# Second layer of a four-layer attention kernel: turns of one pair of heads of both batches, turned probabilities in the scores' banks

## The chip, the cores and the metric

The kernel runs on one core of a Trainium2 chip. The metric is the device time of one execution in microseconds (us); several runs are made, and their median is given.

## The reference

Four cross-attention layers run one after another over `x` of shape (16, 128, 256), each with the same context `ctx_2048` of that shape. The change touches the second layer alone. It handles 16 batches with 16 heads of 64 rows each; its weights differ for the first and the second half of the 256 columns:

```python
for i in range(len(IDX_LIST)):                      # columns 0:128 and 128:256
    s, e = (bounds[i], bounds[i + 1])
    h = jnp.einsum('od,bdl->bol', Wq_list[i], z1ss[:, :, s:e])
    h = h + jnp.einsum('od,bdl->bol', Wi_list[i], u1ss[:, :, s:e])
    chunks.append(h)
w_heads = jnp.concatenate(chunks, axis=2)
q, k, v = jnp.split(w_heads, 3, axis=1)             # 16 heads of 64 rows each
rq = q + r_w_bias[None, :, :, None]
score = jnp.einsum('bndi,bndj->bnij', rq, k) * SCALE
prob = jax.nn.softmax(score, axis=-1)
attn_vec = jnp.einsum('bnij,bndj->bndi', prob, v)
attn_vec = attn_vec.reshape(bsz, N_HEAD * D_HEAD, qlen)
attn_out = jnp.einsum('od,bdl->bol', Wo, attn_vec) + bo[None, :, None]
x = attn_out + z1ss
m = jnp.mean(x, axis=1, keepdims=True)
var = jnp.var(x, axis=1, keepdims=True)
return (x - m) * jax.lax.rsqrt(var + LN_EPS)
```

The first layer (self attention, cross attention and an MLP) runs before it; the third and fourth layers run after it and overlap its end.

## The kernel before, in words

The second layer is `layers123`, and every engine has a program of its own in it that waits on counted semaphores. The 16 batches go in 8 **rounds** of NB = 2 batches. A round has PAIRS = 8 pairs of heads, and STEPS = 16 **steps**: step t handles pair t // 2 of batch t % 2, so each step is two heads of one batch.

What happens to one step, with the function that does it and its line:

- `project` (L1797 for v, L1799 for q and k, on TensorE, PE in the profile) makes q and k of a pair for both batches, or v of four heads for one batch. Each call is 12 matmuls over the full 128 x 128 array, of 256 columns each. The values that are multiplied are split into a rounded part and a rest ("h" and "l" in the tiles' names), hence three products for each one. ScalarE (ACT) rounds q and k out of PSUM into `qh`, `kh` (`round_work`, L1954, L1957), VectorE (DVE) makes the rests (`rest_work`, L2045, L2049) and copies v (L2040). Two PSUM banks, 6 and 7, take these projections and the small matmuls of the layer norm in turn (`work`).
- `scores` (L1813): 12 matmuls per step, each with 64 rows of the array, those of the two heads at the same time in the two halves. They go to `score_bank`, PSUM banks 0 and 1, one for each head.
- `maxima` (L2018, DVE), `exponentials` (L1934, ACT, with the sums), `inverse_sums` (L2024, DVE), `norm` (L1739, GpSimd, POOL).
- `turn` (L1825): 8 transposes of 128 x 128 blocks of the probabilities, over the full array, into `turn_bank`, banks 2 and 3. `copy_turned` brings them to `pT`: head 0 on ACT (L1943), head 1 on DVE (L2029).
- `times_v` (L1841): the probabilities times v, each matmul with 64 columns of the array, the two heads at the same time, into `pv_bank`, half of bank 4. ACT rounds the result (`round_heads`, L1949), DVE makes its rest (`rest_heads`, L2034).
- `times_wo` (L1850): once a pair, three matmuls of 512 columns into bank 5, which adds up over the whole round.

TensorE's order is written by hand in `body`: in step t, `scores(t)`, `times_v(t - 2)`, `turn(t - 1)`, in even steps `times_wo` of the pair two behind, and then the calls that the table `FILLS` names for the step, one to three of them. These fills are the projections of the next pair and the layer norm of the round before: "mean" (L1859), "var" (L1866) and "inv0", "inv1" (`spread`, L1874). `T_Y`, `T_READ`, `T_DIAG` and `T_ZU` are the steps in which the other engines do the round's extra work: adding the residual, the inverse root, the diagonal, and splitting the next round's inputs into `zu` (L1963 and L1968 on ACT, L2055 and L2060 on DVE). In the first round ACT, DVE and POOL also split the weights in parts (`round_part`, `rest_part`).

Since the scores of every step use the same two banks, `scores(t)` waits until the exponentials of step t - 1 have been read:

```python
pe.wait_ge(*exp_done.at(i, 2 * t - 1))
```

`turn(t)` waits for `norm` of its step and for `copy_turned` of step t - 1, `times_v(t)` for both `copy_turned` of its step and for `rest_heads` of step t - 1.

Of the kernel before, what the change touches and what calls it, by code (L numbers as in the profile page):

```python
# [9 lines left out]
F32 = mybir.dt.float32  # L10
# [5 lines left out]
P = 128  # L16
B = 16
D = 256
# [1537 lines left out]
def layers123(nc, v):  # L1556
# [8 lines left out]
    RE = 2  # L1565

    L_T, L_V, L_W = 1, 2, 4
    SCALE = HD1 ** -0.5
    with ExitStack() as ctx:
# [33 lines left out]
        q = [sb(f"q{p}", [P, 2, 2, NB, P], F32R) for p in ("h", "l")]  # L1603
        k = [sb(f"k{p}", [P, 2, 2, NB, P], F32R) for p in ("h", "l")]
        vs = sb("vs", [P, 2, NB, 2, 4 * HD1])
        prob = sb("prob", [P, RE, 2, BANK])
        pT = sb("pT", [P, 2, BANK])
# [51 lines left out]
        FILLS = [("q1", "k1"), ("v0b1", "q2"), ("k2",), ("v1b0", "q3"), ("k3", "v1b1"), ("q4", "mean"), ("k4",),  # L1659
                 ("v2b0", "q5", "var"), ("k5",), ("v2b1", "q6"), ("k6", "v3b0"), ("q7", "k7"), ("v3b1", "inv0"),  # L1660
                 ("inv1",), ("q0+", "k0+"), ("v0b0+",)]
        T_Y, T_CENTRE, T_READ, T_DIAG, T_ZU = 2, 6, 8, 9, 13
# [14 lines left out]
        pv_done = event("pv_done", STEPS)  # L1677
        aT_hi = event("aT_hi", STEPS)
        aT_lo = event("aT_lo", STEPS)
# [7 lines left out]
        joins = {"work_free": [work.out(n, R1 - 1) for n in ("inv0", "inv1")], "product_free": y_done.at(R1),  # L1687
                 "scores_free": ((exp_done.at(R1 - 1, 2 * STEPS - 1),),
                                 tuple(copied[h].at(R1 - 1, STEPS - 1) for h in range(2)))}
# [15 lines left out]
        def tile_of(name):  # L1705
            slot = int(name[1]) % 2
            if name[0] == "v":
                return vs[:, slot, int(name[3]), :, :].rearrange("p c f -> p (c f)")
            return [w[:, slot, :, :, :].rearrange("p c b l -> p (c b l)") for w in (q if name[0] == "q" else k)]
# [25 lines left out]
        def _(pool):  # L1735
# [18 lines left out]
            def body(i, first, last):  # L1754
                for t in range(STEPS):
                    for h in range(2):
                        norm(i, t, h)
                    if first and t < len(PARTS) - AT_ONCE:
                        rest_part(t + AT_ONCE)
                    if t == T_READ:  # L1760
                        inverse_std(i, "var")
# [18 lines left out]
        def _(pe):  # L1780
# [21 lines left out]
            def scores(i, t):  # L1802
# [422 lines left out]
```

## Time and profile before

| What | Value |
|---|---|
| median of 3 runs | 1278.05 us (1273.24 to 1278.2) |
| the profiled execution's own time | 1274.89 us |
| its span | 1273.2 us |
| busy in the span: PE, DVE, ACT, POOL | 95%, 73%, 65%, 43% |
| first and last matmul of `scores` start at | 466.5 and 1188.7 us |

The span is what the hardware profiler recorded of the core, and 1.7 us lie around it. A PE row gives the time at which a matmul starts and a modelled length that overlaps the next one: matmuls of a steady stream start 0.11 to 0.12 us apart while each is listed with 0.28 us. Whether TensorE lost time is therefore read from the starts. "x8" in a row of the timeline means that eight like instructions are merged, and the time is that of all of them.

### The profile page before, as it was taken

What the parts mean: (1) busy time and instruction counts of PE and PEld (TensorE: products, weight loads), DVE (VectorE), ACT (ScalarE), POOL (GpSimd) and SP (SyncE); (2) the same over time, 40 slices, a digit from 0 to 9 for tenths busy, and PEclk for the clock granted to TensorE, in tenths of its full rate; (3) what the DMA queues carried; (4) which work ended last, traced back from release to release, by engine and by line L of the source; (5) the groups of instructions that cost most, each with busy time, mean ns of one, the idle gap of its engine ahead of it and who ended that gap; (6) DMA issues with size and microseconds to landing.
All of it is one profiled execution on the core that took longest, in us unless ns stands there. A gap on an engine that the chain in (4) does not pass through costs nothing.

```text
span 1273.2 us, 29851 instructions
## 1 busy us (share of the span) xinstructions
PE 1204.5 (95%) x10914; PEld 989.7 (78%) x10914; DVE 927.0 (73%) x1835; ACT 825.9 (65%) x2523; POOL 547.2 (43%) x535
## 2 busy tenths in 40 slices
PE   4789999999999889999999999999999999999997
PEld 3667787788887678888888888888888888888675
DVE  4778989889898658767676766767667676766564
ACT  4688978978986658565655565565565656655542
POOL 4455655556643236433333334333334334333443
PEclk8999999999999999999999999999999999999999
DMA  3350000000000000000000000000000100000011
GB/s 108 101 211 16 10 22 9 12 12 17 6 14 1 1 25 2 1 10 2 1 10 2 9 2 1 10 1 2 9 2 2 55 1 2 1 2 1 18 42 42
DMA packets 18575, 25.39 MB, mean 20 GB/s; under 512 B 1424, under 2 KB 17040, under 8 KB 17936
## 3 DMA queue, kind: packets, MB, share of 16 engines
q1 hardware_dynamic: 18448, 23.69, 5.6%
q8 instruction: 81, 1.33, 0.4%
q14 instruction: 46, 0.38, 0.1%
HBM read 21.58 MB, written 2.10 MB: 19 GB/s over the span
## 4 chain that ended last, share of the span: by engine, by line
PE 51%; ACT 6%; DVE 3%; issue 2%; DMA 0%; POOL 0%; ACTq 0%; SPq 0%
PE psum L1797 12%; PE psum L1841 9%; PE psum L1825 9%; PE psum L1813 7%; PE psum L1799 5%; ACT prob L1934 3%; PE psum L1850 3%; ACT pT L1943 1%; PE psum L1322 1%; PE psum L1386 1%; DVE l_neg_max L2018 1%; DVE aTl L2034 1%; PE psum L1866 1%; PE psum L1336 1%; ACT aTh L1949 1%
## 5 line engine op out<-in xcount | busy, mean ns | idle before, releaser
L1739 POOL TENSOR_TENSOR prob<-prob,l_z_inv 128x512 f32<-128x512 f32 x256 | 261.0, 1040 | 439.1 <-DVE l_z_inv L2024 439.1
L1934 ACT ACTIVATE prob<-psum,l_neg_max 128x256 f32<-128x256 f32 x512 | 235.5, 472 | 225.7 <-DVE l_neg_max L2018 225.7
L794 ACT ACTIVATE ring_e<-ring_e,neg_max 128x128 f32<-128x128 f32 x512 | 164.2, 406 | 15.0 <-DVE neg_max L973 14.9
L2018 DVE TENSOR_REDUCE l_neg_max<-psum 128x2 f32<-128x512 f32 x256 | 163.8, 681 | 10.7 <-PE psum L1813 10.6
L1825 PEld LDWEIGHTS psum<-ident,prob 128*128 128x128 f32 x1024 | 109.8, 141 | 50.3 <-issue 45.4
L1841 PE MATMUL psum<-pT,vs 128*64 128x256 f32 x1024 | 138.8, 391 | 3.7 <-DVE aTl L2034 3.5
L1825 PE MATMUL psum<-ident,prob 128*128 128x128 f32 x1024 | 140.2, 280 | 1.0 <-POOL prob L1739 1.0
L478 POOL TENSOR_TENSOR ring_e<-ring_e,cross_add 128x512 f32<-128x512 f32 x64 | 85.2, 1348 | 90.4 <-DVE ring_e L968 90.4
L2029 DVE COPY pT<-psum 128x512 f32<-128x512 f32 x128 | 88.0, 687 | 45.6 <-PE psum L1825 45.4
L478 POOL TENSOR_TENSOR ring_e<-ring_e,self_add 128x512 f32<-128x512 f32 x64 | 85.9, 1356 | 62.6 <-DVE ring_e L968 61.9
L2034 DVE TENSOR_TENSOR aTl<-psum,aTh 128x256 fp32r<-128x256 f32 x128 | 54.3, 424 | 74.6 <-ACT aTh L1949 74.6
L802 ACT COPY ring_t<-psum 128x512 f32<-128x512 f32 x128 | 75.2, 588 | 45.7 <-PE psum L645 44.9
L1934 ACT ACTIVATION_READ_ACCUMULATOR prob<-psum,l_neg_max 128x1 f32 x512 | 103.9, 203 | 0.0
L1841 PEld LDWEIGHTS psum<-pT,vs 128*64 128x64 f32 x1024 | 63.6, 136 | 39.6 <-issue 7.3
L645 PE MATMUL psum<-ident,ring_e 128*128 128x128 f32 x512 | 81.6, 283 | 10.3 <-ACT ring_t L802 9.3
L1813 PE MATMUL psum<-kh,qh 64*128 64x256 f32 x512 | 85.8, 329 | 5.4 <-ACT prob L1934 5.4
L645 PEld LDWEIGHTS psum<-ident,ring_e 128*128 128x128 f32 x512 | 61.5, 144 | 34.4 <-issue 13.3
L973 DVE TENSOR_REDUCE neg_max<-ring_e 128x4 f32<-128x512 f32 x128 | 84.7, 673 | 2.3 <-POOL ring_e L478 2.3
L1943 ACT COPY pT<-psum 128x512 f32<-128x512 f32 x128 | 76.3, 596 | 0.2 <-PE psum L1825 0.2
L1813 PE MATMUL psum<-kl,qh 64*128 64x256 f32 x512 | 72.8, 278 | 0.0
L1813 PE MATMUL psum<-kh,ql 64*128 64x256 f32 x512 | 72.5, 276 | 0.0
L1797 PE MATMUL psum<-zuh,wzl 128*128 128x256 f32 x256 | 72.2, 282 | 0.0
(208 smaller groups left out, 3169.9 us busy)
## 6 DMA issues: line engine op xcount, KB each, us to landing
wz_raw<-wz_in SPq DMA_DIRECT2D x2, 1536.0 KB, 14.6
wi_raw<-wi_in SPq DMA_DIRECT2D x2, 1536.0 KB, 19.2
x_in<-x SPq DMA_DIRECT2D x8, 256.0 KB, 2.7
cT<-ctxT SPq DMA_DIRECT2D x8, 256.0 KB, 2.8
w<-w_in SPq DMA_DIRECT2D x2, 1024.0 KB, 8.9
l_ub<-ctx_in SPq DMA_DIRECT2D x8, 256.0 KB, 3.2
cg<-ctx_in SPq DMA_DIRECT2D x4, 512.0 KB, 4.1
out<-fin SPq DMA_DIRECT2D x8, 256.0 KB, 2.2
```

The costliest lines, as they stand in the source:

```text
L478: pool.tensor_tensor(e, e, add, ALU.add).then_inc(scores_add.sem, 1)
L645: last = nc.tensor.transpose(turn_bank[:, h * P:(h + 1) * P], ring_e[:, n % RE, h * P:(h + 1) * P], ident[:, :])
L794: last = nc.scalar.activation(e, e, ACT.Exp, bias=neg_max[:, n % RE, h:h + 1])
L1739: pool.tensor_tensor(e, e, z_inv[:, t % RE, h, :].unsqueeze(2).broadcast_to([P, 2, D]), ALU.mult)\
L1797: last = mm(o, w, zu[xp][:, s, c, :, :].rearrange("p b l -> p (b l)"), **flags)
L1813: last = mm(score_bank[h][:, qt * D:(qt + 1) * D], q[qp][rows, pair % 2, qt, b, :], k[kp][rows, pair % 2, :, b, :], start=(qp, kp) == (0, ...
L1825: last = nc.tensor.transpose(turn_bank[h][:, kt * D + qt * P:kt * D + (qt + 1) * P], prob[:, t % RE, h, qt * D + kt * P:qt * D + (kt + 1) ...
L1841: last = mm(pv_bank[h * HD1:(h + 1) * HD1, :], vs[:, pair // 2 % 2, b, kt, at:at + HD1], pT[:, h, kt * D:(kt + 1) * D], start=kt == 0, sto ...
L1934: last = nc.scalar.activation(prob[:, t % RE, h, qt * D:(qt + 1) * D], score_bank[h][:, qt * D:(qt + 1) * D], ACT.Exp, bias=neg_max[:, t % ...
L1943: nc.scalar.copy(pT[:, 0, :], turn_bank[0]).then_inc(copied[0].sem, 1)
L2018: nc.vector.tensor_reduce(neg_max[:, t % RE, h, :], score_bank[h].rearrange("p (t c) -> p t c", t=2), AX.X, ALU.max, negate=True).then_inc ...
L2029: nc.vector.tensor_copy(pT[:, 1, :], turn_bank[1]).then_inc(copied[1].sem, 1)
```

## The change

A round now has 8 **turns** n, one for each pair of heads, each with both batches. The scores of batch 0 go to banks 0 and 1 and those of batch 1 to banks 2 and 3. There are no banks of their own for the turned probabilities: `turn` of pair n - 1 and batch b writes into the banks in which the scores of pair n and batch b stood, once the exponentials have read them. The order on TensorE in turn n is: `scores(n, 0)`, `scores(n, 1)`, `times_v(n - 2)` for both batches, the first fill, `turn(n - 1, 0)`, the second fill, `times_wo(n - 2)`, `turn(n - 1, 1)`, the other fills. `pv_bank` is the whole of bank 4, so `round_heads` and `rest_heads` run once a pair over 512 columns. `prob` has four slots (RE = 4) and `pT` one for each batch; `q` and `k` have one slot in place of two. The other engines' orders follow. Where the last round meets the third layer, the waits name the new events, and `queries_keys3` and `values3` come after the last turn.

```diff
-    RE = 2
+    RE = 4
...
-        score_bank = [psum[:, j, :] for j in range(2)]
-        turn_bank = [psum[:, 2 + j, :] for j in range(2)]
-        pv_bank = psum[:, 4, 0:D]
+        score_bank = [[psum[:, 2 * b + h, :] for h in range(2)] for b in range(NB)]
+        pv_bank = psum[:, 4, :]
...
-        T_Y, T_CENTRE, T_READ, T_DIAG, T_ZU = 2, 6, 8, 9, 13
+        FILLS = [("q1", "k1", "v0b1"), ("q2", "k2", "v1b0"), ("q3", "k3", "v1b1", "mean"),
+                 ("q4", "k4", "v2b0", "var"), ("q5", "k5", "v2b1"), ("q6", "k6", "v3b0", "inv0"),
+                 ("q7", "k7", "inv1", "v3b1"), ("q0+", "k0+", "v0b0+")]
+        T_Y, T_READ, T_DIAG, T_ZU = 1, 3, 4, 6
...
+            def scores(i, n, b):
...
-                pe.wait_ge(*exp_done.at(i, 2 * t - 1))
+                for h in range(2):
+                    pe.wait_ge(*copied[h].at(i, NB * (n - 2) + b))
...
+            def turn(i, n, b):
+                t = NB * n + b
                 for h in range(2):
                     pe.wait_ge(*probs_done.at(i, 2 * t + h))
-                    pe.wait_ge(*copied[h].at(i, t - 1))
...
+                        pe.wait_ge(*exp_done.at(i, 2 * (t + NB) + h))
...
+            def body(i, first, last):
+                for n in range(PAIRS):
+                    f = fills(i, n, last)
+                    scores(i, n, 0)
+                    scores(i, n, 1)
+                    if n >= 2 or not first:
+                        times_v(*behind(i, n, 2))
+                    fill(f[0:1])
+                    if n >= 1 or not first:
+                        turn(*behind(i, n, 1), 0)
+                    fill(f[1:2])
...
+                        times_wo(*behind(i, n, 2))
+                    if n >= 1 or not first:
+                        turn(*behind(i, n, 1), 1)
+                    fill(f[2:])
...
+                    exponentials(i, n, 0, 0)
+                    exponentials(i, n, 0, 1)
+                    if n >= 2 or not first:
+                        round_heads(*behind(i, n, 2))
+                    if f:
+                        round_work(f[0][1], f[0][0])
+                    exponentials(i, n, 1, 0)
+                    if n >= 1 or not first:
+                        copy_turned(*behind(i, n, 1), 0)
+                    exponentials(i, n, 1, 1)
+                    if f:
+                        round_work(f[1][1], f[1][0])
+                    if n >= 1 or not first:
+                        copy_turned(*behind(i, n, 1), 1)
```

How the instructions stand on TensorE in a middle round (`kh,qh` and the like are `scores`, `pT,vs` is `times_v`, `ident,prob` is `turn`, `wzh` and `zuh` are projections, `woh` is `times_wo`). A step before:

```order
L1813 MATMUL psum<-kh,qh 128x256 [waits l1_exp_done]
...
L1813 MATMUL psum<-kh,ql 128x256 x2
L1841 MATMUL psum<-pT,vs 64x256 [waits l1_pT1_copied,l1_aT_lo,l1_pT0_copied,l1_work_bank1_read_out]
L1841 MATMUL psum<-pT,vs 64x256 x3
L1825 MATMUL psum<-ident,prob 128x128 [waits l1_pT0_copied,l1_probs_done]
```

A turn after the change, up to the first transposes:

```order
L1820 MATMUL psum<-kh,qh 128x256 [waits l1_pT0_copied,l1_pT1_copied,l1_work_bank0_read_out,l1_work_bank1_read_out]
...
L1820 MATMUL psum<-kh,qh 128x256 [waits l1_pT1_copied,l1_pT0_copied]
...
L1820 MATMUL psum<-kh,ql 128x256 x2
L1853 MATMUL psum<-pT,vs 64x256 [waits l1_pT1_copied,l1_pT0_copied,l1_aT_lo]
...
L1801 MATMUL psum<-zuh,wzh 128x256 [waits l1_work_bank0_read_out,l1_zu_lo,i_weights_lo_made,z_weights_lo_made]
...
L1836 MATMUL psum<-ident,prob 128x128 [waits l1_exp_done,l1_probs_done]
```

The sequence scores, times v, full array came twice a pair and comes once; the scores no longer wait for exponentials, and the transposes now do.

ScalarE (ACT) in a middle turn after the change, from `round_heads` to the second `copy_turned`:

```order
L1971 CAST aTh<-psum 128x512 [waits l1_wo_done,l1_pv_done]
L1976 ACTIVATE qh<-psum,cols 128x512 [waits l1_work_bank1_full]
L1957 ACTIVATE prob,l_z_sum<-psum,l_neg_max 128x256 [waits l1_turned,l1_max_done]
...
L1966 COPY pT<-psum 128x512 [waits l1_pv_done,l1_turned]
L1957 ACTIVATE prob,l_z_sum<-psum,l_neg_max 128x256 [waits l1_turned,l1_max_done]
...
L1979 ACTIVATE kh<-psum 128x512 [waits l1_work_bank0_full]
L1966 COPY pT<-psum 128x512 [waits l1_pv_done,l1_turned]
```

The rounding of q, which waits for its projection, now stands in front of the two exponentials of batch 1; before, the rounding of q or k closed a step.

## Rows read from the trace of the kernel before

**Rows 1.** Windows: stretch and length, busy PE, PEld, DVE, ACT, POOL, PEclk, DMA, GB/s
```profile
863.00:954.00 91.00, 89.79 (x777) 75.24 (x777) 62.63 (x133) 53.46 (x177) 33.59 (x33) 1.00 0.02 5
```

**Rows 2.** Timeline of PE (start, us, line): the "mean" of two rounds
```profile
863.53 1.02 PE L1859 MATMUL psum<-l_y,mean_w 128*128 128x512 f32 x2
...
954.87 1.02 PE L1859 MATMUL psum<-l_y,mean_w 128*128 128x512 f32 x2
```

**Rows 3.** Timeline of PE, one step without a stall
```profile
852.41 0.28 PE L1797 MATMUL psum<-zul,wih 128*128 128x256 f32 x1
852.53 0.28 PE L1797 MATMUL psum<-zuh,wil 128*128 128x256 f32 x1
852.74 0.39 PE L1813 MATMUL psum<-kh,qh 64*128 64x256 f32 x2
852.96 0.28 PE L1813 MATMUL psum<-kl,qh 64*128 64x256 f32 x2
...
853.43 0.28 PE L1813 MATMUL psum<-kh,ql 64*128 64x256 f32 x2
853.64 1.08 PE L1841 MATMUL psum<-pT,vs 128*64 128x256 f32 x8
854.66 1.09 PE L1825 MATMUL psum<-ident,prob 128*128 128x128 f32 x8
855.51 0.47 PE L1850 MATMUL psum<-aTh,woh 128*128 128x512 f32 x1
...
856.28 0.28 PE L1797 MATMUL psum<-zuh,wzh 128*128 128x256 f32 x1
```

**Rows 4.** The same step, asked for in shorter windows: later starts in `times_v`
```profile
853.91 0.60 PE L1841 MATMUL psum<-pT,vs 128*64 128x256 f32 x4
...
854.12 0.60 PE L1841 MATMUL psum<-pT,vs 128*64 128x256 f32 x4
```

**Rows 5.** Timeline of PE in the first layer: full-array matmuls, then transposes
```profile
100.94 1.03 PE L556 MATMUL psum<-lnT,wq 128*128 128x256 f32 x4
101.81 0.60 PE L645 MATMUL psum<-ident,ring_e 128*128 128x128 f32 x4
```

**Rows 6.** Timeline of PE: the two kinds of stall in a round
```profile
909.65 0.31 PE L1813 MATMUL psum<-kh,ql 64*128 64x256 f32 x2
910.19 1.08 PE L1841 MATMUL psum<-pT,vs 128*64 128x256 f32 x8 [0.23 <-DVE aTl L2034]
...
919.94 0.28 PE L1799 MATMUL psum<-wil,zuh 128*128 128x256 f32 x1
920.58 0.39 PE L1813 MATMUL psum<-kh,qh 64*128 64x256 f32 x2 [0.35 <-ACT prob L1934]
```

**Rows 7.** Timeline of ACT: rounding of q, exponentials of two heads, copy, cast
```profile
852.84 0.69 ACT L1954 ACTIVATE qh<-psum,cols 128x512 fp32r<-128x512 f32 x1 [0.95 <-PE psum L1797]
...
913.21 0.47 ACT L1934 ACTIVATE prob<-psum,l_neg_max 128x256 f32<-128x256 f32 x1 [2.59 <-DVE l_neg_max L2018]
...
915.02 0.60 ACT L1943 COPY pT<-psum 128x512 f32<-128x512 f32 x1
915.49 0.41 ACT L1949 CAST aTh<-psum 128x256 fp32r<-128x256 f32 x1
915.75 0.73 ACT L1954 ACTIVATE qh<-psum,cols 128x512 fp32r<-128x512 f32 x1
916.34 0.63 ACT L1957 ACTIVATE kh<-psum 128x512 fp32r<-128x512 f32 x1
```

**Rows 8.** By line, 560 to 1100 us: busy us, mean ns of one | idle before
```profile
L2018 DVE TENSOR_REDUCE l_neg_max<-psum 128x2 f32<-128x512 f32 x188 | 120.3, 681 | 7.3 <-PE psum L1813 7.3
```

**Rows 9.** Timeline of DVE: the split of the next round's inputs
```profile
910.14 1.51 DVE L2055 TENSOR_TENSOR zul<-xs,zuh 128x512 fp32r<-128x512 f32 x1
911.57 0.68 DVE L2060 TENSOR_TENSOR zul<-l_ub,zuh 128x512 fp32r<-128x512 f32 x1
```

**Rows 10.** By line, 466 to 560 us: splitting the weights in the first round
```profile
L2102 DVE TENSOR_TENSOR wzl<-wz_raw,wzh 128x256 fp32r<-128x256 f32 x18 | 8.9, 532 | 0.0
```

More of the change, by code:

```diff
@@ L1754, in body @@
             def body(i, first, last):
[L1755 to L1760, printed above, removed]
+                for n in range(PAIRS):
+                    for b in range(NB):
+                        for h in range(2):
+                            norm(i, NB * n + b, h)
+                        t = NB * n + b
+                        if first and t < len(PARTS) - AT_ONCE:
+                            rest_part(t + AT_ONCE)
+                    if n == T_READ:
                         inverse_std(i, "var")
@@ L1876, in spread @@
                 last.then_inc(bank.fills(name), 1)
-            def body(i, first, last):
-                for t in range(STEPS):
-                    scores(i, t)
-                    if t >= L_V or not first:
-                        times_v(i, t - L_V)
-                    if t >= L_T or not first:
-                        turn(i, t - L_T)
-                    if first and t == L_W:
-                        pe.wait_ge(wo_lo_made, 1)
-                    if t % 2 == 0 and (t >= L_W or not first):
-                        times_wo(i, (t - L_W) // 2) if t >= L_W else times_wo(i - 1, (t - L_W) // 2 + PAIRS)
-                    for name, r in fills(i, t, last):
-                        if is_made(name):
-                            project(r, name)
-                        elif name == "mean":
-                            mean(r, name)
-                        elif name == "var":
-                            variance(r, name)
-                        else:
-                            spread(r, name, int(name[3]))
-                    if last and t == STEPS - 2:
-                        queries_keys3(0)
-                    if last and t == STEPS - 1:
-                        values3(0, 0)
-                        values3(0, 1)
@@ new lines, in fill @@
+            def fill(found):
+                for name, r in found:
+                    if is_made(name):
+                        project(r, name)
+                    elif name == "mean":
+                        mean(r, name)
+                    elif name == "var":
+                        variance(r, name)
+                    else:
+                        spread(r, name, int(name[3]))
+            def body(i, first, last):
+                for n in range(PAIRS):
+                    f = fills(i, n, last)
[7 more added lines that the diff above has]
+                    fill(f[1:2])
+                    if first and n == 2:
+                        pe.wait_ge(wo_lo_made, 1)
+                    if n >= 2 or not first:
[3 more added lines that the diff above has]
+                    fill(f[2:])
+                if last:
+                    queries_keys3(0)
+                    values3(0, 0)
+                    values3(0, 1)
@@ L1909, in tail @@
                 values3(1, 0)
-                times_v(i - 1, STEPS - 1)
+                times_v(i - 1, PAIRS - 1)
                 values3(1, 1)
@@ L1975, in body @@
             def body(i, first, last):
[L1976 to L1983 removed]
+                for n in range(PAIRS):
+                    f = fills(i, n, last)
+                    exponentials(i, n, 0, 0)
+                    exponentials(i, n, 0, 1)
+                    if n >= 2 or not first:
+                        round_heads(*behind(i, n, 2))
[9 more added lines that the diff above has]
+                        copy_turned(*behind(i, n, 1), 1)
+                    if n == T_ZU and not last:
                         round_z(i + 1)
                         round_u(i + 1)
[L1986 to L1990 removed]
+                    if first:
+                        for m in range(NB * n, NB * n + NB):
+                            if m + AT_ONCE < len(PARTS):
+                                round_part(m + AT_ONCE)
             read_queries_keys3, exponentials3, step3, end3 = scalar3(act)
```

213 lines of the change are left out of this document (109 added, 104 removed).

## The prediction

> **What bounds the kernel now.** I read the windows first, then TensorE's timeline by starts, then ACT's and DVE's timelines for what could take its place. In the second layer TensorE is busy for 89.79 of 91 us, while DVE has 62.63, ACT 53.46 and POOL 33.59, and PEclk is 1.00, which is the upper of the two clock levels, 2.4 GHz [rows 1]. So no other engine sets the pace, and what TensorE does not have to do comes off the end. A round takes 954.87 - 863.53 = 91.34 us [rows 2], and the layer has eight.
>
> "Busy" hides small holes, because a matmul's listed length overlaps the next. The starts show them. Two full-array projections start 0.12 apart, and the doublets of the scores (852.96 to 853.43 in four intervals) as well [rows 3]. Around the narrow groups it looks different [rows 3, 4]:
> - from the last projection to the first scores 0.21 in place of 0.12, and to the second doublet of scores 0.22 in place of 0.12: **0.09 + 0.10**.
> - from the last scores to the first `times_v` 0.21 in place of 0.12: **0.09**.
> - `times_v` has four doublets. A middle interval is 854.12 - 853.91 = 0.21, so four are 0.84, yet 1.02 pass until the first transpose: **0.18**.
>
> That is 0.46 us each time the array goes from full matmuls to those with 64 rows, to those with 64 columns, and back. Changes between groups that both use the full array are free: in the first layer four matmuls start at 100.94 and the transposes behind them at 101.81, which is 4 x 0.217 and nothing more [rows 5], and the three matmuls of `times_wo` and the projection behind them follow at the pace of their columns [rows 3]. Those changes have semaphore waits too, so the hole belongs to the change of shape and not to the wait.
>
> The second loss is stalls. Behind a step with short fills, `scores` comes at 0.64 after the last projection in place of 0.21, because the exponentials of the step before still read the same two banks (ACT's `prob`): 0.43. The `times_v` of such a step comes at 0.54 in place of 0.21 because `aTl` is late: 0.33 [rows 6]. Each kind occurs twice a round, at the two steps named by the table as ("v3b1", "inv0") and ("q0+", "k0+") or beside them: 2 x 0.43 + 2 x 0.33 = **1.5 us** a round.
>
> **The change, part by part.**
>
> *Fewer changes of shape.* The scores of both batches stand together, and so do the two `times_v`. Sixteen passes through the three shapes in a round become eight. Gain 8 x 0.46 = **3.7 us** a round. The matmuls themselves are as many as before. The trace does not show scores behind scores of another bank; the nearest row is doublet behind doublet within one group [rows 3], with no hole. That is the value taken. The other bound is that the semaphore wait between them brings back the 0.09 of an entry, twice a turn: 1.4 us less a round.
>
> Here a rule of the Trainium skill would give less. "TensorEngine Tiling (Array Packing)", Key Properties, says that changing the tiling mode drains the array, and "TensorE: Matmul & The Clock Gate", step-by-step phases, puts a drain at about 128 cycles. At 2.4 GHz that is an estimate of 0.053 us for a change, 24 changes fewer a round would bring 1.3 us, and the whole forecast would be some 19 us less of a gain. The trace agrees that only a change of shape costs something, but its holes are two to three times as long (0.46 us over three changes); the rows decide.
>
> *The old stalls.* `scores(n, b)` now waits for the copies of turned probabilities of the turn before, and `times_v(n - 2)` for a rest made one turn earlier. Both are whole groups of matmuls away. Gain **1.5 us** a round. With nothing gained here the round would lose those again; this is an end of the range.
>
> *The transposes' new wait.* `turn(n - 1, b)` needs the exponentials of (n, b). I follow one turn from the start of its scores. TensorE: scores of batch 0 until 0.9 (0.19 + 6 x 0.12), batch 1 until 1.6, both `times_v` until 3.5 (0.09 + 8 x 0.21 + 0.15), q until 5.0 (12 x 0.12), first turn until 5.8 (0.85), k until 7.3, `times_wo` until 8.0 (0.77), and the second head of the second turn at 8.5. Without a v or a layer-norm fill behind it a turn would end at 8.9; with v it is 10.3. ACT: scores of batch 0 are handed on at 1.1 (0.2, from the 0.31 between the start of the last projection and the rounding of q [rows 7]); one maximum of 0.68 [rows 8] brings the first exponential to 1.8; two heads take 1.81 [rows 7], until 3.6; `round_heads` over 512 columns about 0.5, as the copy's spacing is 0.47, until 4.2; then ACT waits for q until 5.2. That is a cover of 1.0. From there rounding q 0.59, a head 0.9, the copy 0.47, a head 0.9 and a hand-over of 0.2 [rows 7] give 8.3 against 8.5. **So the second transposes just make it, with 0.2 to spare**. I take zero in an ordinary turn; the ends are a gain of nothing, and a loss of 0.2 a turn if two or three of the hand-overs take 0.1 more than read.
>
> The cover breaks once a round. In the turn after the inputs are split, ACT's cast comes first and DVE then needs 1.43 + 0.68 us [rows 9] before its first maximum: it starts at about 2.9 and not at 1.1. Of the 1.8 late, 1.0 + 0.2 are covered: **0.6 us lost** a round. The two passes of the mean, one by 512 columns each, make the maxima 0.5 late, which is covered.
>
> *DVE, ACT and POOL.* One cast and one rest of 512 columns replace two of 256; this takes from engines that wait anyway and counts nothing. DVE's four maxima in a row put `inverse_sums` later, and POOL's four norms with it, but turn n's are wanted only in turn n + 1, some 10 us on. Cover: the whole turn.
>
> *The first round.* DVE also makes the rests of weight parts, four operations of 0.53 a turn [rows 10] = 2.1 us in turns 1 to 3, ahead of the maxima. Like the split of the inputs this exceeds the cover by some 0.6: +2 us in all. POOL's part now waits for ACT in the middle of a turn; the norms behind it still have a turn's time. *The end.* In the last turn no projection stands between scores and transposes. TensorE reaches the second head of the second turn at 0.9 + 0.7 + 1.9 + 0.85 + 0.77 + 0.43 = 5.6, while ACT, no longer waiting for q, is there at 4.2 + 0.9 + 0.47 + 0.9 + 0.2 = 6.7: +1.1 us.
>
> **The sum.** A later round: -3.7 - 1.5 + 0.6 = -4.6, seven times -32.2. The first round: -3.7 - 1.5 + 2 = -3.2. The end: +1.1. Together -34.3. The profiled execution took 1274.9, so 1240.6, rounded to **1241 us**. The median of the three runs is 3 us above that execution, the fastest run 2 us below it; I leave the number where the sum puts it.
>
> **The rivals.**
> 1. *The exponentials become TensorE's wait, and it is slower.* Place: ACT's row q, head, copy, head in front of the second transposes. Every 0.1 us beyond the slack of 0.2 costs 64 x 0.1 = 6.4 us, as nothing on TensorE can move past the wait. The gain of 34 is gone at 0.54 us beyond the slack in every turn. At 0.7 the time is 1241 + 45 = 1286. For: the slack is the smallest number in this text, and a late turn hands its lateness to `copy_turned`, which the next scores need. Against: every duration in the row is from a row of the same engine, the next scores have 0.9 us of their own to wait for k, and ACT is busy for 53 of 91 us.
> 2. *The same wait, mild.* 0.2 us a turn: +13, so 1254.
> 3. *The holes belong to the groups' waits and not to the shapes.* Then scores behind scores and `times_v` behind `times_v` keep them, and only the stalls go: 8 x (1.5 - 0.6) less 3 = 4 us, 1271. Against: the free changes with waits [rows 3, 5].
> 4. *More is gained.* The first transposes behind `times_v` also start slowly, which I have not counted, and no turn loses 0.6. If a shape pass is worth 0.55 and both new losses are nil: 8 x (4.4 + 1.5) = 47, 1228.
>
> That the change does not do what it says is hardly possible; the order on TensorE shows both groupings.
>
> **How the numbers follow.** Forecast (within 1232 to 1250) 0.60; rival 4, 0.12; rival 2, 0.13; rival 3, 0.07; rival 1, 0.05; anything else that leaves the time where it was, 0.03. Range: from 1230, inside rival 4, to 1257, beyond rival 2, with 0.15 left outside for the two slow ones and about 0.05 below. What a measurement of this kernel can tell from no change is about 0.5%, 6 us. Faster by more than that: 0.60 + 0.12 + 0.13 + half of rival 3 and a little = 0.90; the same 0.04; slower 0.06.
>
> **What would show each step.** The period of the "mean" falls from 91.3 to 86 or 87 us. In a turn, scores of batch 1 follow those of batch 0 at 0.12, and the second `times_v` the first at 0.21. TensorE's idle entries for `prob` before scores vanish. Entries for `prob` before the transposes appear once a round, in the turn after the inputs are split, with some 0.6 us. If they appear in every turn, rival 1 or 2 holds; if scores behind scores show 0.2, rival 3.

## The result, and the profile of the changed kernel

| What | Before | After |
|---|---|---|
| median, measured together | 1276.68 us (4 runs) | 1246.35 us (1245.56 to 1247.28, 4 runs) |
| ratio, 95% interval | | 0.9768 (0.9748 to 0.9788) |
| profiled execution, its span | 1274.89, 1273.2 us | 1245.98, 1244.2 us |

The change makes the kernel 2.3% faster. The forecast was 1241 us, between 1230 and 1257. Against its own base, the profiled execution, it promised 34.3 us and 28.9 came.

The page's busy time by engine, of the kernel before and of the changed one:

```profile
PE 1204.5 (95%) x10914; PEld 989.7 (78%) x10914; DVE 927.0 (73%) x1835; ACT 825.9 (65%) x2523; POOL 547.2 (43%) x535
```
```profile
PE 1176.8 (95%) x10914; PEld 989.1 (79%) x10914; DVE 908.0 (73%) x1771; ACT 818.7 (66%) x2459; POOL 551.7 (44%) x535
```

The shares are those of before, within a point, and show nothing of the 29 us. TensorE's busy time itself is 27.7 us less for the same 10914 matmuls, because a modelled length covers a small hole as if it were work. The window of a middle round (columns as in [rows 1]) is now busy throughout, where 1.2 of 91 us were idle, and the clock is still the upper one:

```profile
848.00:934.00 86.00, 86.00 (x777) 75.20 (x776) 59.63 (x125) 52.93 (x170) 33.60 (x34) 1.00 0.02 5
```

The starts show it. Timeline of TensorE after the change: the first scores of rounds one and two, a middle turn, and the "mean" of two rounds:

```profile
467.39 0.39 PE L1820 MATMUL psum<-kh,qh 64*128 64x256 f32 x2
...
557.56 0.39 PE L1820 MATMUL psum<-kh,qh 64*128 64x256 f32 x2
...
826.91 0.28 PE L1803 MATMUL psum<-wil,zuh 128*128 128x256 f32 x1
827.12 0.39 PE L1820 MATMUL psum<-kh,qh 64*128 64x256 f32 x2
827.34 0.28 PE L1820 MATMUL psum<-kl,qh 64*128 64x256 f32 x2
...
827.82 0.28 PE L1820 MATMUL psum<-kh,ql 64*128 64x256 f32 x2
827.94 0.28 PE L1820 MATMUL psum<-kh,qh 64*128 64x256 f32 x2
...
828.53 0.28 PE L1820 MATMUL psum<-kh,ql 64*128 64x256 f32 x2
828.74 1.95 PE L1853 MATMUL psum<-pT,vs 128*64 128x256 f32 x16
830.62 0.39 PE L1801 MATMUL psum<-zuh,wzh 128*128 128x256 f32 x1
...
847.92 0.59 PE L1872 MATMUL psum<-l_y,mean_w 128*128 128x512 f32 x1
...
934.29 0.59 PE L1872 MATMUL psum<-l_y,mean_w 128*128 128x512 f32 x1
```

- A round is 934.29 - 847.92 = 86.37 us where it was 91.34 [rows 2]: 4.97 less (forecast 4.6).
- Batch 1's scores follow batch 0's at 0.12 (827.82, 827.94), though they stand behind semaphore waits of their own. Into the scores (826.91, 827.12) it is still 0.21 in place of 0.12, and so it is into `times_v` (828.53, 828.74).
- Both `times_v` are eight doublets in 1.88 us, 0.235 each. Before, four took 1.02 [rows 3].

The span, cut where both traces can be cut. The first scores of the last pair start at 1183.01 before and at 1151.69 after.

| Stretch | Before | After | Change | Forecast |
|---|---|---|---|---|
| to the first scores | 466.46 | 467.39 | +0.9 | 0 |
| first round | 88.74 | 90.17 | +1.4 | -3.2 |
| then, to the last turn | 627.8 | 594.1 | -33.7 | -32.2 |
| last turn to the end | 90.2 | 92.5 | +2.3 | +1.1 |
| span | 1273.2 | 1244.2 | -29.0 | -34.3 |

The third stretch stops one turn before the end of the seven rounds that the forecast's -32.2 is for. Seven whole rounds at 4.97 would be 34.8, so the middle delivered a little more than was promised, and the first round gave 4.6 us of it back.

The +0.9 ahead of the first scores is not clear of what differs from run to run. The nine kernels of the runs below are like one of these two up to there, and their first scores start anywhere from 465.26 to 467.57.

The first and the last row also hold different work. `times_v` now runs two pairs behind the scores where it ran two steps, one pair, behind, and the transposes run a pair behind where they ran one step. So the first round has 96 matmuls of `times_v` and 112 transposes where it had 112 and 120, and the last stretch has 48 and 32 where it had 32 and 24. At the paces of the changed kernel (1.88 us for sixteen, 0.79 for eight) that is 2.7 us that moved from the first round to the end. The forecast counted it in neither; in the span it cancels.

The waits of TensorE (us in all, times, longest). Before, 560 to 1180 us:

```profile
PE psum L1813 <- ACT prob L1934: 4.2, 12, 0.4
...
PE psum L1841 <- DVE aTl L2034: 2.8, 12, 0.2
```

After, the same question for 560 to 1150 us gives no row at all: for seven rounds no wait is listed. The list leaves out the shortest gaps (an experiment below has some of 0.1 us), but the starts agree: in a middle round every two transposes of a group stand 0.11 apart. For 466 to 540 us the answer has this row:

```profile
PE psum L1836 <- ACT prob L1957: 6.8, 12, 1.9
```

So the transposes do wait for the exponentials, but only in the first round, and once more in the very last turn. The first round's turns take 7.55, 9.65, 14.20, 14.07, 12.05, 10.89, 11.31 and 10.45 us. The third, fourth and fifth take 11.31, 11.24 and 10.46 in a later round, so these three alone are 7.3 us too long. The worst of these waits, on TensorE:

```profile
491.65 0.63 PE L1836 MATMUL psum<-ident,prob 128*128 128x128 f32 x4 [1.86 <-ACT prob L1957]
...
505.79 0.63 PE L1836 MATMUL psum<-ident,prob 128*128 128x128 f32 x4 [1.80 <-ACT prob L1957]
```

DVE ahead of them, where four rests of weight parts stand before the maxima (a third group of four takes 3.78 ahead of the fifth turn's):

```profile
485.31 4.06 DVE L2134 TENSOR_TENSOR wzl<-wz_raw,wzh 128x256 fp32r<-128x256 f32 x4
...
489.83 2.41 DVE L2050 TENSOR_REDUCE l_neg_max<-psum 128x2 f32<-128x512 f32 x4
...
500.65 3.34 DVE L2134 TENSOR_TENSOR wzl<-wz_raw,wzh 128x256 fp32r<-128x256 f32 x4
```

and by line for 466 to 560 us, the answer to [rows 10]:

```profile
L2134 DVE TENSOR_TENSOR wzl<-wz_raw,wzh 128x256 fp32r<-128x256 f32 x18 | 14.3, 844 | 0.0
```

The forecast took 2.1 us for four of them, from the 532 ns of before. Now they take up to 4.06, with POOL at work at the same moment (an experiment below shows that this is why):

```profile
484.42 1.43 POOL L1753 TENSOR_TENSOR wil<-wi_raw,wih 128x256 fp32r<-128x256 f32 x2 [2.16 <-ACT wih L1995]
485.81 2.40 POOL L1741 TENSOR_TENSOR prob<-prob,l_z_inv 128x512 f32<-128x512 f32 x2
488.17 1.79 POOL L1753 TENSOR_TENSOR wil<-wi_raw,wih 128x256 fp32r<-128x256 f32 x2
```

The same effect with the other sign fits what the turn behind the input split shows, which lost nothing (10.45 us like an ordinary one). DVE after the change:

```profile
806.99 0.69 DVE L2087 TENSOR_TENSOR zul<-xs,zuh 128x512 fp32r<-128x512 f32 x1
807.60 0.68 DVE L2092 TENSOR_TENSOR zul<-l_ub,zuh 128x512 fp32r<-128x512 f32 x1
...
811.37 0.69 DVE L2067 TENSOR_TENSOR aTl<-psum,aTh 128x512 fp32r<-128x512 f32 x1 [0.31 <-ACT aTh L1971]
```

The first was 1.51 us before [rows 9]. POOL then had a norm beside it; after the change POOL's norms end at 805.7, and it starts the next at 810.83. POOL before the change, and after it:

```profile
909.06 2.04 POOL L1739 TENSOR_TENSOR prob<-prob,l_z_inv 128x512 f32<-128x512 f32 x2 [3.47 <-DVE l_z_inv L2024]
```
```profile
804.70 1.04 POOL L1741 TENSOR_TENSOR prob<-prob,l_z_inv 128x512 f32<-128x512 f32 x1 [1.10 <-DVE l_z_inv L2057]
...
810.83 2.04 POOL L1741 TENSOR_TENSOR prob<-prob,l_z_inv 128x512 f32<-128x512 f32 x2 [5.08 <-DVE l_z_inv L2057]
```

### The profile page after: what moved, and what is told of

It is laid out like the page before. It is cut to its first block, busy times and chain, and to the rows that moved or that the text cites. A ratio compares the mean times of both kernels' runs of the same rounds, so it can differ in the third digit from the quotient of the medians.

```text
span 1244.2 us, 29755 instructions
## 1 busy us (share of the span) xinstructions
PE 1176.8 (95%) x10914; PEld 989.1 (79%) x10914; DVE 908.0 (73%) x1771; ACT 818.7 (66%) x2459; POOL 551.7 (44%) x535
## 4 chain that ended last, share of the span: by engine, by line
PE 57%; ACT 2%; DVE 2%; issue 1%; DMA 0%; SPq 0%; ACTq 0%
PE psum L1801 14%; PE psum L1853 9%; PE psum L1836 9%; PE psum L1820 8%; PE psum L1803 7%; PE psum L1863 3%; ACT prob L1957 2%; PE psum L1322 1%; PE psum L1386 1%; DVE wzl L2134 1%; PE psum L1336 1%; PE psum L1887 1%; PE psum L1872 1%; PE psum L1879 1%; PE psum L1364 1%
## 5 line engine op out<-in xcount | busy, mean ns | idle before, releaser
L2050 DVE TENSOR_REDUCE l_neg_max<-psum 128x2 f32<-128x512 f32 x256 | 158.7, 683 | 11.2 <-PE psum L1820 11.1
L1836 PE MATMUL psum<-ident,prob 128*128 128x128 f32 x1024 | 134.5, 273 | 7.1 <-ACT prob L1957 7.1
L1836 PEld LDWEIGHTS psum<-ident,prob 128*128 128x128 f32 x1024 | 116.8, 141 | 19.3 <-issue 9.9
L1853 PE MATMUL psum<-pT,vs 128*64 128x256 f32 x1024 | 124.6, 385 | 0.0
L2081 DVE SCALAR_TENSOR_TENSOR kl<-psum,kh 128x512 fp32r<-128x512 f32 x64 | 44.3, 692 | 87.3 <-ACT kh L1979 87.3
L1853 PEld LDWEIGHTS psum<-pT,vs 128*64 128x64 f32 x1024 | 67.8, 136 | 36.7 <-issue 0.7
L2077 DVE SCALAR_TENSOR_TENSOR ql<-psum,cols,qh 128x512 fp32r<-128x512 f32 x64 | 48.1, 751 | 46.7 <-ACT qh L1976 45.8
L1820 PE MATMUL psum<-kh,qh 64*128 64x256 f32 x512 | 78.9, 305 | 0.6 <-issue 0.6
L1976 ACT ACTIVATE qh<-psum,cols 128x512 fp32r<-128x512 f32 x64 | 44.2, 690 | 45.2 <-PE psum L1801 44.3
L1801 PE MATMUL psum<-zuh,wzh 128*128 128x256 f32 x224 | 73.6, 329 | 0.0
```

What stands on the lines that cost most here:

```text
L1801: last = mm(o, w, zu[xp][:, s, c, :, :].rearrange("p b l -> p (b l)"), **flags)
L1820: last = mm(score_bank[b][h][:, qt * D:(qt + 1) * D], q[qp][rows, qt, b, :], k[kp][rows, :, b, :], start=(qp, kp) == (0, 0), stop=(qp, kp) ...
L1836: last = nc.tensor.transpose(score_bank[b][h][:, kt * D + qt * P:kt * D + (qt + 1) * P], prob[:, t % RE, h, qt * D + kt * P:qt * D + (kt + ...
L1853: last = mm(pv_bank[h * HD1:(h + 1) * HD1, b * D:(b + 1) * D], vs[:, n // 2 % 2, b, kt, at:at + HD1], pT[:, b, h, kt * D:(kt + 1) * D], st ...
L2050: nc.vector.tensor_reduce(neg_max[:, t % RE, h, :], score_bank[b][h].rearrange("p (t c) -> p t c", t=2), AX.X, ALU.max, negate=True).then_ ...
```

## The experiments

All times are medians beside runs of the kernel before on the same chip. That kernel's median was 1275.3 to 1275.4 there and 1276.68 beside the changed kernel, so a difference from the changed kernel's 1246.35 is good to about 1.5 us. Edits are to the changed kernel if nothing else is said.

| Run | Median (range, runs) | Ratio to before (95%) |
|---|---|---|
| weight parts behind the maxima | 1237.29 (1236.71 to 1238.1, 5) | 0.9702 (0.9689 to 0.9715) |
| POOL's weight parts later | 1239.85 (1237.82 to 1242.0, 5) | 0.9728 (0.9712 to 0.9744) |
| `times_v` split | 1259.66 (1259.14 to 1263.29, 4) | 0.9888 (0.9873 to 0.9903) |
| ACT chain longer | 1272.63 (1270.08 to 1274.71, 10) | 0.9979 (0.997 to 0.9989) |
| order on ACT only | 1270.63 (1269.3 to 1274.56, 5) | 0.9973 (0.9953 to 0.9992) |
| before, k moved | 1282.16 (1281.87 to 1284.92, 5) | 1.0061 (1.0048 to 1.0075) |
| before, v moved | 1271.7 (1271.0 to 1274.04, 10) | 0.9976 (0.9966 to 0.9985) |
| first run, and the end filled | 1237.27 (1236.47 to 1238.46, 5) | 0.9705 (0.9691 to 0.9719) |
| both orders of parts, end filled | 1238.6 (1238.19 to 1239.68, 5) | 0.9714 (0.97 to 0.9728) |

**The first round: weight parts behind the maxima.** In DVE's turn the rests of the weight parts move from the end of the turn before to the place behind the four maxima (the parts are grouped anew by one on the way):

```diff
                     maxima(i, n, 1, 0)
                     maxima(i, n, 1, 1)
+                    if first and n > 0:
+                        for m in range(NB * n, NB * n + NB):
+                            if m < len(PARTS):
+                                rest_part(m)
...
-                    if first:
-                        for m in range(NB * n, NB * n + NB):
-                            if 0 < m <= len(PARTS) - AT_ONCE:
-                                rest_part(m - 1 + AT_ONCE)
```

> The changed kernel, with DVE's rests of weight parts in the first round moved from the end of a turn to behind the four maxima of the next one; nothing else differs. Theory (the first round lost its gain because these four operations stand ahead of the maxima and, running beside POOL, take 3.3 to 4.1 us and not 2.1): the eight turns of the first round go from 90.2 us to 84 to 86, the two holes of 2.1 us ahead of the first transposes vanish, and the kernel comes to 1240 to 1242, against 1246.4 for the change. L2134 takes about 0.45 us each where POOL is idle. Rival (ACT's casts or POOL's parts are what the first round waits for): the first round stays within 1 us of 90.2, and the time at 1245 to 1247.

First scores of rounds one and two in this kernel:

```profile
467.31 0.39 PE L1820 MATMUL psum<-kh,qh 64*128 64x256 f32 x2
...
549.73 0.39 PE L1820 MATMUL psum<-kh,qh 64*128 64x256 f32 x2
```

The first round takes 82.4 us instead of 90.2, and the later ones stay at 86.37. The span falls by 7.8, which is all of it from here, and more than the theory had expected. The parts themselves are also faster in the mean (by line, 466 to 560 us):

```profile
L2134 DVE TENSOR_TENSOR wzl<-wz_raw,wzh 128x256 fp32r<-128x256 f32 x18 | 8.7, 537 | 0.0
```

So this run shows that the first round's loss comes from the parts ahead of the maxima, but not whether their place or their slowness is at fault. No other kernel here is clearly faster.

**Place or contention: POOL's parts later.** DVE's order is left alone; in the first round POOL makes its parts one turn later, between the norms of batch 0 and those of batch 1, in place of `rest_part(t + AT_ONCE)` behind each batch:

```diff
-                        t = NB * n + b
-                        if first and t < len(PARTS) - AT_ONCE:
-                            rest_part(t + AT_ONCE)
+                        if first and n > 0 and b == 0:
+                            for m in range(NB * n, NB * n + NB):
+                                if m < len(PARTS):
+                                    rest_part(m)
```

> The changed kernel, with DVE's weight parts left at the end of the turn, ahead of the maxima, but POOL's parts moved one turn later, behind its first two norms. So POOL no longer works beside DVE's parts for most of their time. Theory (DVE's operations are slow there because POOL runs beside them): the four of them fall from 3.3 to 4.1 us to 1.8 to 2.4, the maxima of turns 2 and 3 start 1.5 to 2 us sooner, the holes ahead of the first transposes shrink by as much, and the first round goes from 90.2 to 85 to 87 us; the kernel to 1241 to 1244. Rival (only their place counts, and their length belongs to the operation itself): four still take 3.3 us or more, first round 89 or more, 1245 to 1247.

DVE in this kernel:

```profile
483.06 2.27 DVE L2135 TENSOR_TENSOR wzl<-wz_raw,wzh 128x256 fp32r<-128x256 f32 x4
...
496.19 1.42 DVE L2135 TENSOR_TENSOR wzl<-wz_raw,wzh 128x256 fp32r<-128x256 f32 x4
```

The same four operations in the same place take 2.27 and 1.42 us instead of 4.06 and 3.34. The first round runs from 465.26 to 549.56, 84.3 us, and TensorE's waits for `prob` in it fall from 6.8 to 1.5 us. Of the 7.8 us that the first run took off the first round, 5.9 go without any change of place on DVE, by less contention with POOL (none of TensorE's waits in that round was for POOL itself). The profiled execution, 1237.89 us, is 8.1 below the changed kernel's, but 2.1 of it lie ahead of the first scores and are not the edit's: from 30 to 100 us this trace shows a granted clock of 0.98, where all others have 0.92 to 0.94. The median is 6.5 below.

**The shapes: `times_v` split.** The two batches' `times_v` stand apart again, with the projection of q between them; ACT rounds q before the heads, and DVE makes its rest first:

```diff
-                        times_v(*behind(i, n, 2))
+                        times_v(*behind(i, n, 2), 0)
                     fill(f[0:1])
+                    if n >= 2 or not first:
+                        times_v(*behind(i, n, 2), 1)
...
```

> The changed kernel, with the projection of q put between the times_v of batch 0 and that of batch 1 (ACT and DVE handle q ahead of the heads' rounding, so that they wait for neither). The matmuls are the same, and the array changes shape twice more a turn: full to 64 columns and back. Theory (the holes belong to the change of shape): the entry costs 0.09 plus a slow first interval of 0.06, the exit 0.10 to 0.18, so 0.25 to 0.3 a turn, the round goes from 86.4 to 88.5 or 88.8, and the kernel from 1246 to 1262 to 1266. Rival (the old holes came from waits and short fills, not from shapes): no new hole, 1245 to 1248.

TensorE in this kernel:

```profile
790.62 1.08 PE L1853 MATMUL psum<-pT,vs 128*64 128x256 f32 x8
791.64 0.39 PE L1801 MATMUL psum<-zuh,wzh 128*128 128x256 f32 x1
...
793.05 0.28 PE L1801 MATMUL psum<-zuh,wil 128*128 128x256 f32 x1
793.26 1.08 PE L1853 MATMUL psum<-pT,vs 128*64 128x256 f32 x8
794.27 0.44 PE L1836 MATMUL psum<-ident,prob 128*128 128x128 f32 x2
```

An ordinary turn takes 10.73 us instead of 10.45, with no wait for ACT between 560 and 1150 us. Two more changes of shape, full array to 64 columns and back, cost 0.28. The rows carry 0.24 of it: the two halves take 1.02 + 1.01 instead of 1.88, and the second is entered at 0.21 (793.05, 793.26) instead of 0.12. The rest is at the transposes behind it: the first two are listed together with 0.44, so they start some 0.16 apart where it is 0.11 elsewhere. The round is 88.37, 2.0 us more, and the kernel 13 us slower, a little less than expected.

**The slack: ACT's chain longer.** Four copies into a spare tile, before the exponentials of batch 1:

```diff
                         round_work(f[0][1], f[0][0])
+                    for j in range(4):
+                        nc.scalar.copy(spare[:, 32 * j:32 * j + 32], ident[:, 32 * j:32 * j + 32])
                     exponentials(i, n, 1, 0)
```

> The changed kernel, with four small copies (128 x 32) to a spare tile on ACT between the rounding of q and the exponentials of batch 1, in every turn. They do nothing for the result. From the old trace they should take 0.15 to 0.2 us each, 0.6 to 0.8 together. Theory (the second transposes are only 0.2 us behind the exponentials that they wait for): each turn grows by what the copies take beyond 0.2, so by 0.4 to 0.6, a round by 3.2 to 4.8, and the kernel by 25 to 38 us to 1271 to 1284, with TensorE waiting for ACT's prob in every turn. Rival (ACT has cover to spare, as its busy share of 66% suggests): within 3 us of 1246.

ACT, the transposes of the second head of batch 1, and TensorE's waits between 560 and 1150 us, in this kernel:

```profile
791.61 0.56 ACT L2008 COPY l_spare<-ident 128x32 f32<-128x32 f32 x4
792.08 0.47 ACT L1958 ACTIVATE prob<-psum,l_neg_max 128x256 f32<-128x256 f32 x1
```
```profile
794.36 0.62 ACT L1980 ACTIVATE kh<-psum 128x512 fp32r<-128x512 f32 x1
```
```profile
794.64 0.63 PE L1837 MATMUL psum<-ident,prob 128*128 128x128 f32 x4 [0.21 <-ACT prob L1958]
```
```profile
PE psum L1837 <- ACT prob L1958: 10.6, 52, 0.2
```

The copies hold ACT for 792.08 - 791.61 = 0.47 us, and an ordinary turn becomes 10.83, 0.38 more. So the slack is about 0.09. The listed waits (10.6 us) hold about half of the loss; the starts hold all of it. The hand-over shows too: ACT goes on to `kh` at 794.36, the transposes start at 794.64, so it takes 0.28 us.

**The same by order alone.** Only ACT's order and DVE's are changed, as in the split above: q is rounded before the heads, so that the heads' cast stands between q and the exponentials of batch 1. No work is added. The part on ACT:

```diff
+                    if f:
+                        round_work(f[0][1], f[0][0])
                     if n >= 2 or not first:
                         round_heads(*behind(i, n, 2))
-                    if f:
-                        round_work(f[0][1], f[0][0])
...
```

> The changed kernel with only the other half of the split run: ACT and DVE handle q ahead of the heads' rounding and its rest, and TensorE's order is as changed. It separates the two edits of that run. Theory (the 0.28 us a turn of the split run belong to the shapes): ordinary turns stay at 10.45 us, unless ACT, which now waits for q at 5.2 us and rounds the heads afterwards, is later by the 0.5 us of that rounding; then each turn grows by about 0.4, to 10.8, and TensorE waits for ACT's prob, which the split run did not. Either way TensorE's gaps between scores, times_v and q stay as in the changed kernel. Rival (the order of ACT and DVE itself makes the split run's holes at times_v): gaps of 0.2 to 0.3 beside times_v.

ACT in this kernel:

```profile
777.37 0.69 ACT L1976 ACTIVATE qh<-psum,cols 128x512 fp32r<-128x512 f32 x1 [1.15 <-PE psum L1801]
777.96 0.58 ACT L1971 CAST aTh<-psum 128x512 fp32r<-128x512 f32 x1
778.42 0.49 ACT L1957 ACTIVATE prob<-psum,l_neg_max 128x256 f32<-128x256 f32 x1
```

and TensorE from `times_wo` on:

```profile
779.50 0.50 PE L1863 MATMUL psum<-aTh,woh 128*128 128x512 f32 x1
779.84 0.40 PE L1863 MATMUL psum<-aTl,woh 128*128 128x512 f32 x1
...
780.31 1.32 PE L1836 MATMUL psum<-ident,prob 128*128 128x128 f32 x8
```

One cast that holds ACT for 778.42 - 777.96 = 0.46 us, moved across q, makes every ordinary turn 0.40 longer: a slack of 0.06. No wait is listed between 560 and 1150 us, and yet the eight transposes take 1.32, where the changed kernel has 1.04. DVE's later rest adds 0.1 between the first two matmuls of `times_wo` (0.34 apart, 0.23 elsewhere); it costs nothing of its own, since the transposes of the second head start 8.86 us into the turn here and 8.85 in the run with the copies, against 8.49. The edit gives back 24 us or more of the 30 of the whole change. Two edits of different kinds agree on a slack of 0.06 to 0.09.

**Can the old order lose its stalls by moving fills?** I had put the stalls of [rows 6] down to the short fills of the step before. In the kernel before, one fill is moved in the table of the last steps:

```diff
-("q0+", "k0+"), ("v0b0+",)]
+("q0+",), ("k0+", "v0b0+")]
```

> The kernel before, with one entry of its table moved: the projection of the next round's k0 from step 14 to step 15, so that step 15 has two projections and step 14 one beside times_wo. Theory (an odd step with one short fill makes the next scores wait for the exponentials, 0.43 us, and the times_v behind it for its rest, 0.33): one of the two pairs of stalls a round goes, the round falls from 91.3 to 90.6, and the kernel from 1276.7 by 6 us to 1270 or 1271. Rival (the stall is only moved to step 15's own scores, behind the now shorter step 14): within 1.5 us of the kernel before.

TensorE in this kernel:

```profile
826.66 0.39 PE L1813 MATMUL psum<-kh,qh 64*128 64x256 f32 x2 [0.79 <-ACT prob L1934]
...
827.96 1.08 PE L1841 MATMUL psum<-pT,vs 128*64 128x256 f32 x8 [0.32 <-DVE aTl L2034]
```

It is slower, the round 92.38. The stall in front of step 0 stays, and one of 0.79 is new in front of step 15. The rival had named that place, but had the whole within 1.5 us of the kernel before; the run is 7 us above it. In step 14 DVE first splits the inputs and comes to its maxima some 2 us late; the two fills were the cover for that. My account by the length of a step's own fills falls; what must be covered is what DVE and ACT do in that step.

The second edit to the kernel before moves "v3b1" one step on, next to "inv1":

```diff
-("v3b1", "inv0"),
-                 ("inv1",),
+("inv0",),
+                 ("v3b1", "inv1"),
```

> The kernel before with v3b1 moved in its table from step 12 to step 13, so that the step with nothing but inv1 gets a projection too. Theory, after the first moved entry made things slower (a step's cover is what stands between two scores, and the sum over steps is fixed; taking work from one step opens a stall there): the stall in front of step 14 vanishes (-0.75 with that of times_v), and step 12, left with times_wo and inv0, makes step 13 wait by 0.3 to 0.8. The round changes by less than 0.5 us either way, the kernel by less than 4 us. Rival (the stall is the short step's alone): round down by 0.75 us, the kernel by 6 us.

The round is 90.9, 0.44 less, and the kernel 0.24% faster, as the theory had it. Both stalls of step 14 are gone, those of step 0 stay, and a new one stands in step 13:

```profile
721.32 1.08 PE L1841 MATMUL psum<-pT,vs 128*64 128x256 f32 x8 [0.29 <-DVE aTl L2034]
```

Of the 1.5 us a round these two orders of the old kernel win back at best a third. That no other order would do better wasn't tried.

**The end.** The third layer's first work is put in the last turn, where the projections would be, on top of the first run:

```diff
                     fill(f[0:1])
+                    if last and n == PAIRS - 1:
+                        queries_keys3(0)
...
                     fill(f[1:2])
+                    if last and n == PAIRS - 1:
+                        values3(0, 0)
```

and `values3(0, 1)` behind `fill(f[2:])`.

> The kernel with DVE's parts behind the maxima (1237.3), and besides in the last turn of all the third layer's queries_keys3 ahead of the first turn of probabilities and values3(0, 0) ahead of times_wo, where the projections of q and k stand in other turns. Theory (the last turn has nothing between scores and transposes, so TensorE waits some 1.1 us for ACT's exponentials and DVE's rest): the idle entries of 0.39 and 0.28 us there vanish and the end is 1 to 2 us shorter, 1235.5 to 1236.5. Rival (the third layer's own chain from its first scores sets the end): within 0.5 us of 1237.3.

The changed kernel's last turn has waits of 0.39 for `aTl` and 0.28 for `prob`. They go, and this one comes:

```profile
1151.44 1.13 PE L1322 MATMUL psum<-wvpg,cg 128*128 128x256 f32 x4 [0.98 <-ACT l_qk L1426]
```

The stretch from the last turn on is 0.3 us shorter (92.27 against 92.53), and the medians are equal, as the rival had it. The third layer's values need `l_qk`, which ACT makes only behind the second copy of turned probabilities, and for that copy it waits 0.92 us for the transposes itself; the hole changed its place.

**All three together**, with POOL's parts later as well:

> Both moves of the kernel before this one, and POOL's parts one turn later as well. Theory: with DVE's parts already where POOL is idle there is little left for POOL's move to give: within 1 us of the run with the filled end, so 1235 to 1236.5. Rival (POOL's parts still hold up norms that the transposes wait for in the first round): 1 to 2 us less, 1234 to 1235.

The median is 1238.60, 1.3 us above the run with the filled end; neither theory nor rival holds. DVE's parts are now at 418 ns in the mean, yet the first round is 84.0 instead of 82.4: the second turn takes 10.08 instead of 8.67, as a projection waits 1.2 us and starts at 484.29. What it waits for the profile gives only as "issue". POOL starts its four rests of that turn at 482.76 and needs 2.81 us for them, so two are done at about 484.2; that the projection waits for these is likely and not shown.

## Why the prediction was right

**Fewer changes of shape (-3.7 a round): right, measured -3.5.** The saving of a round is 4.97; with the stalls' 1.5 out of it 3.5 remain, 0.43 for each of eight passes against the 0.46 read. The split `times_v` gives one part by itself, 0.28 where the holes of [rows 3, 4] say 0.09 + 0.18. The 0.18 was read a little too large: four doublets more take 1.88 - 1.02 = 0.86, so a middle interval is 0.215 and the hole 0.16; the slow first transposes, which were left out, make up for it. Rival 3, that the holes belong to the waits, falls by the 0.12 between the two batches' scores. Of rival 4 one part came, no turn of a later round lost anything, but a pass was not worth its 0.55. The drain rule of the Trainium skill that the prediction weighed ("TensorEngine Tiling (Array Packing)", Key Properties, with the length from "TensorE: Matmul & The Clock Gate"), an estimate of 0.053 us for a change, would have been too small by a factor of two to three.

**The old stalls (-1.5): right.** By the starts they were 2 x 0.42 and 2 x 0.30 a round, 1.4, and TensorE now has no entry for `aTl` or `prob` in seven rounds. The reason that I gave for them, the short fills, was only half of it, as the first run on the kernel before shows.

**The transposes' wait (slack 0.2, cost nothing): right in sign, close to the edge.** The slack is 0.06 to 0.09. The hand-over from ACT to the transposes was taken as 0.2 and is 0.28. Rivals 1 and 2 had the right mechanism and the right price: 0.38 to 0.40 us beyond the slack, 64 times, is 24 to 26 us, and the two runs lost 26 and 24. The change did not set them off, by a margin of less than 0.1 us, which is as much as the reading could be wrong by; that part was luck. What decided was one choice in the change, the heads' cast in front of q's rounding.

**The turn after the input split (+0.6 a round): did not occur.** The term used 1.43 us for the first subtraction, out of a row with a POOL norm beside it [rows 9]. After the change it is 0.61 from start to start (806.99, 807.60). Of the 1.8 us of lateness 0.8 fall away, and the rest, 1.0, is within the cover of 1.2 that the prediction counted, and still within it with the measured slack (1.1).

**The first round (+2 on it): mis-sized, the step that failed.** -3.2 was forecast and +1.4 came: 4.6 us of the 5.4 between the sum and the profiled execution. The step is "four operations of 0.53 a turn = 2.1 us": they took 4.06, 3.34 and 3.78, so that the exponentials came up to 1.9 us late for the transposes. The term of +2 was 7.3 by the three long turns, and 7.8 by the run that takes the parts out of the way. The 2.7 us of work that moved to the end hid some of it. The mean of 532 ns in [rows 10] was itself a mix (the shortest 409, the median 416, the longest 954), and the change put DVE's parts beside POOL's work. The run with POOL's parts later took 5.9 us of it away.

**The end (+1.1): measured +2.3.** The two waits that the term is about are 0.67. The 2.7 us of moved work are the larger part, and the prediction left them out. Against them stand waits of the old kernel that are gone, its stalls in front of step 14 and in it, and this one:

```profile
1193.16 1.13 PE L1322 MATMUL psum<-wvpg,cg 128*128 128x256 f32 x4 [1.32 <-ACT l_qk L1426]
```

How the rest adds up to +2.3 is not shown. The 0.9 us ahead of the first scores lie within what differs from run to run.

So by the rows of the table the errors were 4.6 in the first round, 1.2 at the end and 0.9 at the start, and the middle gave 1.5 back. That 34.3 stands so near to 28.9 owes something to terms that cancel. The size of the gain came from starts in a steady stretch and held; what failed were durations that depend on what another engine does meanwhile, and stretches that were looked at briefly.

## What to carry to other kernels

Order the matmuls so that groups of one array shape stand together; here each avoided pass through three shapes was worth 0.43 us, though the share of busy time showed nothing. Take a DVE duration from a row in which POOL does what it will do after the change, and put work that is done once behind, not ahead of, the maxima that start the chain. Where a slack comes out at 0.1 or 0.2 us, look at which instruction of another chain stands in that row: one cast on the wrong side of a rounding cost 24 us.

## What the runs showed of the hardware that I had not expected

**DVE beside POOL.** A DVE subtraction of two SBUF tiles, 128x256, ran at 0.36 us each alone (four in 1.42) and at 1.0 beside POOL (four in 4.06); 128x512 took 0.69 and 1.51. An operation with one input in PSUM was not slowed: `aTl` at 811.37 took 0.69 beside POOL's norm of 810.83. POOL pays in some rows and not in others: its two norms beside the weight parts took 2.40 us (485.81), but those beside the input split 2.04 (909.06), as at 810.83. Which pairs contend the Trainium skill states in "SBUF — State Buffer", Who interferes with whom: a DVE instruction with two SBUF inputs contends with a GpSimd instruction that reads SBUF, and one with at most one SBUF input (outside the modes that use both ports) does not. By that rule the trace agrees, with 4.06 against 1.42 us for the first kind and 0.69 for the second. In these rows the factor is 2.2 to 2.9. Weighed in the prediction, the rule would have pointed at the first round's term and at that of the input split.

**Short ACT instructions.** The listed length is not the time that ACT is held: the four spare copies list 0.56 and hold it 0.47, the cast lists 0.58 and holds it 0.46. A chain on ACT is added up from starts.
